# Three PSUM banks for convolutions, one for product sums, one transfer per slot, and a free sequence over all images

## The reference

```python
x = x + _L0_conv_ref(_gn(x), ...)   # gated, oriented 3x3 aggregation
x = x + _L1_conv_ref(_gn(x), ...)   # three plain 3x3 convolutions, 32 -> 64 -> 64 -> 32
```

```python
w = mu * kern
w = w / (jnp.sum(w, axis=(1, 2), keepdims=True) + 1e-06)
agg = jnp.einsum('brsl,bcsl->brcl', w, patches).reshape(Bb, R * C, Hh, Ww)
return jnp.einsum('bkhw,ok->bohw', agg, pw_w) + pw_b[None, :, None, None]
```

## Time and profile before

| | |
|---|---|
| median of 3 runs | 549.23 us (548.38 to 549.37) |
| profiled execution, its own time | 549.03 us |
| its span, first to last instruction | 547.2 us |
| TensorE, VectorE busy | 483.3 us (88%), 419.4 us (77%) |
| ScalarE, GpSimd busy | 216.3 us (40%), 191.4 us (35%) |
| mean granted clock of TensorE | 0.973 of full |

### The profile page before, as it was taken

One profiled execution on the slowest core, in us unless ns is written; L12 is line 12 of the kernel. 1 busy time (PEld: TensorE's weight loads), 2 busy tenths in 40 slices (PEclk: granted clock), 3 DMA queues, 4 the chain that ended last, 5 costly groups with the idle time before them and its releaser, 6 DMA issues.

```text
span 547.2 us, 7160 instructions
## 1 busy us (share of the span) xinstructions
PE 483.3 (88%) x2527; PEld 391.8 (72%) x2527; DVE 419.4 (77%) x553; ACT 216.3 (40%) x408; POOL 191.4 (35%) x95
## 2 busy tenths in 40 slices
PE   2505973789999999999999999999999999998995
PEld 2204752566887788777977797779777987886894
DVE  2598678999898989898989989998989698412211
ACT  1520631265335543643355344644364313340110
POOL 1305524572366117520934083506370542000000
PEclk9999995589999999999999999999999999999999
DMA  4100002430144113421233124321431144024302
GB/s 145 42 1 0 5 0 56 98 72 17 46 97 100 40 38 87 93 59 44 69 95 69 47 53 107 65 55 41 100 77 25 36 95 86 22 56 107 70 5 38
DMA packets 40275, 32.23 MB, mean 59 GB/s; under 512 B 26160, under 2 KB 30768, under 8 KB 40240
## 3 DMA queue, kind: packets, MB, share of 16 engines
q1 hardware_dynamic: 40240, 31.78, 25.1%
HBM read 5.66 MB, written 4.19 MB: 18 GB/s over the span
## 4 chain that ended last, share of the span: by engine, by line
PE 64%; DVE 16%; issue 9%; SPq 4%; ACT 2%; POOL 1%; DMA 1%; DVEq 0%; ACTq 0%; POOLq 0%
PE conv_ps L366 42%; PE agg_ps L427 7%; DVE prod L712 6%; DVE prod L722 5%; PE val_ps L412 5%; SPq L287 4%; PE geo_ps L395 3%; PE geo_ps L386 3%; PE pw_ps L440 2%; PE conv_ps L380 2%; DMA xraw<-in_x 1%; POOL prod L1003 1%; DVE st L546 1%; DVE trig L643 1%; POOL vs L1019 1%
## 5 line engine op out<-in xcount | busy, mean ns | idle before, releaser
L712 DVE TENSOR_TENSOR prod<-val_ps,tapw 128x2048 f32<-128x2048 f32 x80 | 181.0, 2284 | 11.6 <-PE val_ps L412 10.2
L366 PE MATMUL conv_ps<-c_hi,wc_hi 128*128 128x448 f32 (+2 forms) x384 | 157.1, 409 | 0.0
L366 PE MATMUL conv_ps<-c_hi,wc_lo 128*128 128x448 f32 (+2 forms) x384 | 144.6, 376 | 0.0
L366 PE MATMUL conv_ps<-c_lo,wc_hi 128*128 128x448 f32 (+2 forms) x384 | 144.1, 375 | 0.0
L1003 POOL TENSOR_TENSOR prod<-prod 128x2048 f32<-128x2048 f32 x23 | 112.5, 4894 | 16.4 <-DVE prod L712 16.4
L1019 POOL TENSOR_TENSOR vs<-vn 128x1024 f32<-128x1024 f32 x32 | 69.6, 2185 | 74.2 <-ACT vn L843 73.4
L722 DVE TENSOR_TENSOR prod<-prod 128x2048 f32<-128x2048 f32 x35 | 88.7, 2533 | 1.0 <-POOL prod L1003 0.5
L366 PEld LDWEIGHTS conv_ps<-c_hi,wc_hi 128*128 128x128 f32 x384 | 72.5, 189 | 21.7 <-issue 8.3
L366 PEld LDWEIGHTS conv_ps<-c_hi,wc_lo 128*128 128x128 f32 x384 | 72.3, 188 | 10.6
L366 PEld LDWEIGHTS conv_ps<-c_lo,wc_hi 128*128 128x128 f32 x384 | 72.7, 189 | 9.7 <-issue 2.4
L929 ACT ACTIVATE c_hi<-conv_ps 128x512 fp32r<-128x512 f32 (+4 forms) x88 | 41.9, 485 | 86.4 <-PE conv_ps L366 86.2
(11 more groups left out here) (107 smaller groups left out, 506.6 us busy)
## 6 DMA issues: line engine op xcount, KB each, us to landing
xq_hi<-y_hi SPq DMA_DIRECT2D x128, 66.0 KB, 2.0
xq_lo<-y_lo SPq DMA_DIRECT2D x128, 66.0 KB, 2.0
xraw<-in_x SPq DMA_DIRECT2D x32, 128.0 KB, 2.8
x2r<-x SPq DMA_DIRECT2D x128, 32.0 KB, 1.9
out_y<-x2r SPq DMA_DIRECT2D x32, 128.0 KB, 2.8
prod<-in_w SPq DMA_DIRECT2D x1, 576.0 KB, 4.8
vn<-vn SPq DMA_DIRECT2D x16, 24.8 KB, 1.8
prod<-in_w SPq DMA_DIRECT2D x1, 384.0 KB, 3.9
```

Of the source, the lines that this page charges most:

```text
L366: mm = nc.tensor.matmul(bank[:, 0:conv_cols(n)], weights, lo if part == 1 else hi, start=term == part == 0, stop=final and part == 2)
L712: v.tensor_tensor(dst, val.unsqueeze(2).to_broadcast([P, B, R, C]), wgt.unsqueeze(3).to_broadcast([P, B, R, C]), ALU.mult).then_inc(mult_d ...
```

## The change

Four things.

1. `conv_ps` has three banks, `agg_ps` one. A convolution chunk waits for the chunk three back, across images as well. Each of the sums waits until the one before it is copied out.
2. `y_hi` and `y_lo` become two halves of one tensor `y`, `xq_hi` and `xq_lo` of one tensor `xq`, and one transfer carries both halves: 16 transfers per image where there were 32. They wait for `split_low`.
3. `body`, `on` and `run_images` go. Each engine's list is written out step by step for all eight images; the offsets between images differ from image to image, above all at the first two and the last.
4. SP's list has load_x(1) ahead of halo(0), and ScalarE's has the rounding of the convolution weights (`split_weights`) right after norm1(0).

```diff
+N_AGG, N_CONV = 1, 3
-        y_hi = sb("y_hi", [P, 2, K8, PW], F32R)
-        y_lo = sb("y_lo", [P, 2, K8, PW])
+        y = sb("y", [P, 2, 2, K8, PW])
+        y_hi, y_lo = y[:, 0].bitcast(F32R), y[:, 1]
...
         def conv_bank(j, n):
-            return conv_ps[(N_CHUNK * j + n) % 2]
+            return conv_ps[(N_CHUNK * j + n) % N_CONV]
...
-            def by_slots(i, g, low):
+            def by_slots(i, g):
                 if g == 0:
-                    if low:
-                        wait(y_lo_done, i + 1)
-                    else:
-                        wait(y_hi_done, i + 1)
-                        if i >= 1:
-                            wait(conv_done, N_CHUNK * (i - 1) + 4)
-                dst, src = (xq_lo, y_lo) if low else (xq_hi, y_hi)
+                    wait(y_lo_done, i + 1)
+                    if i >= 1:
+                        wait(conv_done, N_CHUNK * (i - 1) + 4)
                 for s in range(4):
                     j0 = (2, 1, 1, 0)[s] + K8 * g
-                    sp.dma_start(dst[C * s:C * s + C, j0:j0 + K8, :].bitcast(F32),
-                                 src[C * g:C * g + C, (s + 1) % 2, :, :].bitcast(F32)).then_inc(xq_in[g], 16)
+                    sp.dma_start(xq[C * s:C * s + C, :, j0:j0 + K8, :].bitcast(F32),
+                                 y[C * g:C * g + C, :, (s + 1) % 2, :, :]).then_inc(xq_in[g], 16)
...
-                    if n >= 2:
-                        if n - 2 < N_SPLIT:
-                            wait_lows(pe, j, n - 1)
-                    elif j >= 1:
-                        pe.wait_ge(out_done, 2 * (j - 1) + n + 1)
+                    before = N_CHUNK * j + n - N_CONV
+                    if before >= 0:
+                        pj, pn = divmod(before, N_CHUNK)
+                        if pn < N_SPLIT:
+                            wait_lows(pe, pj, pn + 1)
+                        else:
+                            pe.wait_ge(out_done, 2 * pj + pn - N_SPLIT + 1)
...
-                if n >= 2 or i >= 1:
-                    pe.wait_ge(agg_sb, 8 * i + n - 1)
+                if 8 * i + n >= N_AGG:
+                    pe.wait_ge(agg_sb, 8 * i + n + 1 - N_AGG)
```

TensorE's new list around the first convolution, and for image 2's sums:

```diff
+            values(1, 6)
+            gn1_sums(2, 1)
+            geometry(2)
+            values(1, 7)
+            v_product(2, 0)
+            values(1, 8)
+            convs(0, 0, 6)
+            v_product(2, 1)
+            take_high(0, 0)
+            take_high(0, 1)
+            transpose_sums(1, 0)
+            convs(0, 6, 10)
+            transpose_sums(1, 1)
+            values(1, 9)
...
+            transpose_sums(2, 3)
+            convs(1, 12, 17)
+            take_high(1, 3)
+            convs(1, 17, 20)
+            pointwise(2, 0)
+            transpose_sums(2, 4)
+            convs(1, 20, 23)
+            transpose_sums(2, 5)
```

VectorE's new list from image 1's first multiplications to image 2's weights:

```diff
+            mult(1, 0)
+            mult(1, 1)
+            mult(1, 2)
+            gn2_stats(0, 0)
+            residual(0, 1)
+            gn2_stats(0, 1)
+            mult(1, 3)
+            mult(1, 4)
+            gn1_stats(2)
+            gn2_spread(0)
+            gn2_scale(0)
+            gn1_spread(2)
+            gn2_bias(0)
+            add_products(1, 0, 2)
+            gn1_scale(2)
+            split_low(0)
+            gn1_bias(2)
+            mult(1, 5)
+            mult(1, 6)
+            tap_weights(2, 0)
+            add_products(1, 0, 3)
```

More of the change, by code:

```diff
@@ L537, in _ @@
[L537 removed]
+                    conv_term(i, k)
+            gn1_sums(0, 0)
+            gn1_sums(0, 1)
+            geometry(0)
+            v_product(0, 0)
+            v_product(0, 1)
+            gn1_sums(1, 0)
+            gn1_sums(1, 1)
+            values(0, 0)
+            values(0, 1)
+            values(0, 2)
+            values(0, 3)
+            geometry(1)
+            values(0, 4)
+            values(0, 5)
+            v_product(1, 0)
+            v_product(1, 1)
@@ new lines, in _ @@
+            values(2, 5)
+            take_high(0, 8)
+            convs(0, 43, 45)
+            gn1_sums(3, 0)
+            convs(0, 45, 46)
+            gn2_sums(1, 1)
+            gn1_sums(3, 1)
+            convs(0, 46, 51)
+            geometry(3)
+            values(2, 6)
+            convs(0, 51, 55)
+            v_product(3, 0)
+            convs(0, 55, 58)
+            v_product(3, 1)
+            values(2, 7)
+            convs(0, 58, 59)
+            transpose_sums(2, 0)
+            convs(0, 59, 60)
@@ new lines, in _ @@
+            values(3, 8)
+            convs(1, 49, 50)
+            gn1_sums(4, 1)
+            convs(1, 50, 57)
+            geometry(4)
+            convs(1, 57, 60)
+            v_product(4, 0)
+            values(3, 9)
+            convs(2, 0, 3)
+            v_product(4, 1)
+            convs(2, 3, 4)
+            transpose_sums(3, 0)
+            convs(2, 4, 7)
+            take_high(2, 0)
+            transpose_sums(3, 1)
+            take_high(2, 1)
+            convs(2, 7, 10)
+            values(4, 0)
@@ new lines, in _ @@
+            take_high(2, 7)
+            gn2_sums(3, 1)
+            take_high(2, 8)
+            values(4, 6)
+            gn1_sums(5, 1)
+            convs(2, 43, 49)
+            geometry(5)
+            convs(2, 49, 53)
+            v_product(5, 0)
+            convs(2, 53, 56)
+            v_product(5, 1)
+            convs(2, 56, 59)
+            values(4, 7)
+            values(4, 8)
+            convs(2, 59, 60)
+            convs(3, 0, 4)
+            transpose_sums(4, 0)
+            convs(3, 4, 5)
@@ new lines, in _ @@
+            convs(3, 53, 54)
+            geometry(6)
+            convs(3, 54, 56)
+            values(5, 8)
+            v_product(6, 0)
+            convs(3, 56, 59)
+            v_product(6, 1)
+            transpose_sums(5, 0)
+            convs(3, 59, 60)
+            convs(4, 0, 4)
+            transpose_sums(5, 1)
+            take_high(4, 0)
+            convs(4, 4, 5)
+            values(5, 9)
+            transpose_sums(5, 2)
+            convs(4, 5, 7)
+            transpose_sums(5, 3)
@@ new lines, in _ @@
+            take_high(4, 7)
+            take_high(4, 8)
+            convs(4, 48, 49)
+            gn1_sums(7, 1)
+            convs(4, 49, 55)
+            geometry(7)
+            convs(4, 55, 56)
+            values(6, 5)
+            transpose_sums(6, 0)
+            v_product(7, 0)
+            values(6, 6)
+            convs(4, 56, 59)
+            transpose_sums(6, 1)
+            values(6, 7)
+            v_product(7, 1)
+            convs(4, 59, 60)
+            convs(5, 0, 1)
+            values(6, 8)
@@ new lines, in _ @@
+            mult(3, 0)
+            mult(3, 1)
+            mult(3, 2)
+            residual(2, 0)
+            mult(3, 3)
+            gn2_stats(2, 0)
+            residual(2, 1)
+            gn2_stats(2, 1)
+            mult(3, 4)
+            mult(3, 5)
+            gn2_spread(2)
+            gn1_stats(4)
+            gn2_scale(2)
+            mult(3, 6)
+            gn2_bias(2)
+            gn1_spread(4)
+            add_products(3, 0, 2)
+            gn1_scale(4)
+            split_low(2)
@@ new lines, in _ @@
+            tap_weights(4, 7)
+            residual(3, 0)
+            mult(4, 0)
+            mult(4, 1)
+            mult(4, 2)
+            gn2_stats(3, 0)
+            residual(3, 1)
+            mult(4, 3)
+            gn2_stats(3, 1)
+            mult(4, 4)
+            gn1_stats(5)
+            gn2_spread(3)
+            gn1_spread(5)
+            gn2_scale(3)
+            gn1_scale(5)
+            gn2_bias(3)
+            mult(4, 5)
+            gn1_bias(5)
+            add_products(4, 0, 2)
```

1182 lines of the change are left out of this document (984 added, 198 removed).

## The result

The changed kernel takes 565.67 us (median; 562.79 to 567.22, 4 runs) against 548.81 (548.25 to 549.37, 4 runs): 3.0% slower, ratio 1.0301, 95% interval 1.0252 to 1.035. The forecast was 538 us, in a range of 531 to 546. The profiled execution took 562.79, with a span of 561.0. It is the fastest of the four, so what is read from its trace explains 13.8 us of the 16.9 between the medians. In what follows medians are over all executions, and ratios leave out those more than 1.5% above the fastest of their kernel (701.54 us, at a granted clock of 0.674, in the old order with fills; 552.86 and 552.91 us with the five waits).

A forecast was written before the change was run, and what follows sets the result against it. TensorE was taken to bound the kernel from the first convolution on, with VectorE close behind. From 549.03 us, - 8.9 (earlier start) + 1.7 (work left) - 7 (third bank) + 3.5 (new waits) gave 538.3, stated as 538; range 531 to 546.

The forecast's parts named there:

- The first convolution: TensorE's start of image 0's convolutions, T0: about 105 us, 8.9 earlier, gated by v_product(2,0) and values(1,8) or y's transfer.
- New waits: TensorE's queue after T0: near misses with VectorE's additions and landings cost some tenths each, 3.5 us in all, bounds 0 and 12.
- Rival C: Port shared by VectorE and GpSimd: VectorE's additions lengthen to up to 4.41 us, total 572 us; chance 0.04.
- The page's rule: SBUF port: VectorE with two SBUF inputs and GpSimd share an exclusive lock, the loser blocked for the other's whole instruction.
- The third bank: Convolution banks: chunks wait for the low part three back, not two; of 11.1 us of TensorE waits, 7 go.
- the work that is left for later: TensorE after T0: sums(1,0..2) and v_product(2,1) now follow it, values(1,8) is done; 1.7 us more.
- One transfer: SP's queue: 16 issues per image, not 32; nothing in the middle, 1.6 us at image 7, T0 105 not 107.
- The single bank: Sums' PSUM bank: spacing never under 0.9 us, so sums aren't held if ScalarE is free; image 0's held about 0.9 each.
- rival D: Single bank of sums: 56 sums, gain gone at 0.2 us held each, 571 us at 0.6; chance 0.06.

The follow-up runs named there:

- the old order with fills: Kernel before, GpSimd's additions of products and pair sums replaced by fills of the same tiles: 545.55 us, 0.9935 of the kernel before.
- the five waits: Changed kernel, GpSimd's first second-half addition of images 0, 1, 2, 4, 5 also waiting for the small VectorE step it held: 547.52 us.
- without GpSimd's reads: Changed kernel, GpSimd's additions of products and pair sums replaced by fills of the same tiles: 536.49 us, 0.9775 of the kernel before.
- the fastest version: Changed kernel with five waits on GpSimd's additions (image 5's one part later), plus waits on second pair sums of images 3 to 6: 543.68 us.

## Why the prediction was wrong

- **The first convolution**: right. 105.88 for 105 us, gated by the two steps named. It could be earlier still: 10.1 us of held time lie ahead of it, and without GpSimd's reads it was at 100.7.
- **New waits, + 3.5 us, bounds 0 and 12**: the step that failed. It followed the queues "with the durations above", those of undisturbed instructions. Measured are 17.8 us of waits in all, where about 5 were before and most should have gone, and 7.7 us of a slower clock behind three of the stalls; the rest of the run is 21.9 us longer than before instead of 1.8 shorter. "Each near miss costs some tenths" was the price of steps that are late by themselves; steps of 0.2 to 0.7 us held for up to 4.4 us were not in it.
- **Rival C** had the mechanism and the wrong victim. It priced the 35 additions at up to 4.41 us; they took 2.30 and never over 2.841. Held were the steps of 0.2 to 0.7 us, and "no long instructions were added on either side" was no argument against it: none was needed, only another neighbour for the same one. A step of 0.28 us held for 4 us costs twice what an addition of 2.28 held to 4.41 does, and it is a link to ScalarE. That TensorE keeps full clock through a stall was also assumed, in silence. The rival's sum came to 572, near the measured 565.67, but by luck: it stood on additions that weren't held.
- **The page's rule.** The Trainium skill, "SBUF — State Buffer", on who interferes with whom, has a VectorE instruction with two SBUF inputs contend with a GpSimd instruction that reads SBUF, and not with one that only writes it. The traces agree: 0.28 us became 4.30 beside an addition of 4.59, and was 0.29 beside fills, which read nothing. I quoted the page in the prediction, and let the sum do without it.
- **The third bank, - 7 us**: too much. With the reads gone in both orders, the stretches from image 1's first convolution to image 7's make 326.5 us against 328.8, and image 7's is 46.1 against 47.2: 3.4 us, with whatever the other edits give or take in it. The first stretch is 3.9 us longer there, where 1.7 was priced for the work that is left for later (with the reads it is 1.8 longer, 60.15 against 58.31). The net there is + 0.5 where - 1.8 (- 5.3 and the + 3.5 of new waits) was forecast.
- **One transfer**: right for the old order (1.6 forecast, 1.5 measured). "In the middle this is worth nothing" was wrong for the new one: it is a condition of it, worth 52 us in the version with the five waits. At the first convolution it is worth 1.2 us (103.94 against 102.78), for 2 forecast. The forecast itself isn't touched by that, since the change has both.
- **The single bank**: right. 0.8 us of waits, under the 3 named, and rival D fell; the cost of a sum that is held is the 0.9 us named.

What stays open: the stretches of 57.6 and 57.9 us in the fastest version still have 3.3 us of held time under pair sums, and the next one 3.9; whether an order without any would come to the 536.5 us of the run without GpSimd's reads wasn't tried.

## What to carry to other kernels

Before pricing a new order, list GpSimd's long instructions that read SBUF and look at what stands next to each in VectorE's queue: beside a multiplication with an input in PSUM they were free here, beside a small step of a chain to TensorE they can cost their own length, and the clock of TensorE on top. Five waits that delayed GpSimd by 0.5 to 3 us were worth 18 us, twice what the earlier start gave. And an edit that is worth 1.5 us in the old order can be what the new one stands on: price it by the lead its transfers have there.

## What the hardware showed that I had not expected

- One-input steps are held too: line 1022's TENSOR_SCALAR from SBUF to SBUF, 0.23 us alone, took over 3 us beside GpSimd's additions at 103.4 and 351.5 us. Fills hold this kind as well: in the new order with fills, line 1027's took 1.83 us, for 0.22 alone.
- Multiplications with one input in PSUM and one in SBUF weren't held at all, 80 of 80 within 2.244 to 2.293 us.
- The granted clock fell to the 1.2 GHz level at each of the three stalls of TensorE of 2.8 to 3.9 us, for some 3 to 7 us, which added 7.7 us to 11.4 of standing. Behind the longest stall of the fastest version, 2.33 us up to 421.14, it stayed at 1.00.
